# Queries of five of eight batches in three 16-bit terms, their normalised rows turned by transposing DMAs, in a fused attention and expert kernel

## The reference

```python
xn = layernorm(x)                               # (8, 256, 256), no gain
q1, q2 = xn @ q1_w.T, xn @ q2_w.T               # the queries of the change
k1, v  = ctx @ kv1_w.T;  k2 = first half of ctx @ kv2_w.T
a = softmax(q1 k1' / 4) - lam * softmax(q2 k2' / 4)
x = x + (rmsnorm(a v) * norm_w) @ proj_w.T + proj_b
x = x + experts(layernorm(x))
```

## Time and profile before

| | |
|---|---|
| median of three runs | 545.44 us (543.28 to 546.12) |
| the profiled execution | 542.85 us, of which the span of the trace is 541.1 us |
| busy share of the span | PE 91%, DVE 71%, ACT 63%, POOL 53% |
| mean granted clock of PE | 0.952 of full |
| data moved | 79.89 MB, DMA queue of SP busy 42.2% of 16 engines |

### The profile page before, as it was taken

One profiled execution on the slowest core, in us unless ns is written; L12 is line 12 of the kernel. 1 busy time (PEld: TensorE's weight loads), 2 busy tenths in 40 slices (PEclk: granted clock), 3 DMA queues, 4 the chain that ended last, 5 costly groups with the idle time before them and its releaser, 6 DMA issues.

```text
span 541.1 us, 12094 instructions
## 1 busy us (share of the span) xinstructions
PE 490.0 (91%) x3720; PEld 364.2 (67%) x3735; DVE 384.6 (71%) x816; ACT 339.7 (63%) x643; POOL 286.0 (53%) x364
## 2 busy tenths in 40 slices
PE   4976989999998988797999999999999999999990
PEld 3845556766765655445778788888888888777650
DVE  5664368998978857794888888888766677666551
ACT  2333688988888886353776777776565556545530
POOL 7332646566546454244146576556656655554244
PEclk9978599999999999697999999999999999999997
DMA  8668676876776534434546877896665555643224
GB/s 258 179 180 257 192 199 184 263 198 191 255 194 190 182 113 147 146 108 132 163 106 137 181 178 153 184 167 165 100 92 95 90 82 94 99 79 61 30 30 50
DMA packets 87883, 79.89 MB, mean 148 GB/s; under 512 B 48456, under 2 KB 73832, under 8 KB 87688
## 3 DMA queue, kind: packets, MB, share of 16 engines
q1 hardware_dynamic: 75900, 62.93, 42.2%
q0 software_dynamic: 11856, 16.16, 18.6%
q10 hardware_dynamic: 68, 0.03, 0.0%
HBM read 49.08 MB, written 22.41 MB: 132 GB/s over the span
## 4 chain that ended last, share of the span: by engine, by line
PE 60%; DMA 11%; DVE 8%; issue 6%; ACT 6%; SPq 6%; POOL 3%; ACTq 0%; POOLq 0%; DVEq 0%
PE bank L1540 26%; PE bank L1559 13%; PE bank L1346 4%; PE bank L1332 3%; SPq L496 3%; PE bank L1297 2%; DMA q_parts<-WE 2%; PE bank L1571 2%; DMA FB<-w 2%; PE bank L1369 2%; PE bank L1355 2%; DMA FB<-x_parts,slot_tok 2%; PE bank L1313 2%; DVE FB L1224 2%; POOL out L749 1%
## 5 line engine op out<-in xcount | busy, mean ns | idle before, releaser
L1540 PE MATMUL bank<-FB,WE 128*128 128x0 bf16 x1440 | 190.2, 283 | 2.4 <-issue 1.6
L1540 PEld LDWEIGHTS bank<-FB,WE 128*128 x1440 | 138.7, 99 | 34.7 <-issue 4.1
L749 POOL DMA_INDIRECT out<-FB,slot_tok x60 | 100.2, 1669 | 87.5 <-DVE FB L1241 82.6
L943 ACT ACTIVATE FB<-FB 128x512 bf16<-128x512 f32 x120 | 75.6, 630 | 68.0 <-DVE FB L1220 64.6
L1224 DVE TENSOR_TENSOR FB<-FB 128x512 bf16<-128x512 f32 x120 | 83.3, 694 | 43.3 <-ACT FB L943 38.6
L1559 PE MATMUL bank<-FB,WE 128*128 128x0 bf16 x720 | 103.5, 280 | 2.9 <-DVE FB L1224 2.4
L1220 DVE TENSOR_TENSOR FB<-FB,bank 128x512 f32<-128x512 f32 x120 | 82.0, 683 | 26.7 <-ACT FB L937 21.5
L937 ACT ACTIVATE FB<-bank 128x512 f32<-128x512 f32 x120 | 70.7, 589 | 34.4 <-PE bank L1540 26.2
L740 POOL DMA_INDIRECT FB<-x_parts,slot_tok x60 | 63.7, 1062 | 52.5 <-DMA FB<-FB 31.6
L1559 PEld LDWEIGHTS bank<-FB,WE 128*128 x720 | 67.7, 98 | 21.8 <-issue 6.3
L656 POOL TENSOR_TENSOR WE<-FB,WE 128x256 bf16<-128x256 f32 x104 | 67.8, 678 | 21.1 <-ACT WE L780 21.1
(11 more groups left out here) (181 smaller groups left out, 612.1 us busy)
## 6 DMA issues: line engine op xcount, KB each, us to landing
FB<-w SPq DMA_DIRECT2D x26, 512.0 KB, 5.4
WE<-w SPq DMA_DIRECT2D x44, 256.0 KB
WE<-q_parts SPq DMA_DIRECT2D x32, 200.0 KB
WE<-x SPq DMA_DIRECT2D x16, 256.0 KB, 5.6
q_parts<-FB SPq DMA_DIRECT2D x32, 128.0 KB
x_parts<-WE SPq DMA_DIRECT2D x20, 128.0 KB, 3.9
out<-WE SPq DMA_DIRECT2D x20, 128.0 KB, 5.0
q_parts<-WE SPq DMA_DIRECT2D x16, 128.0 KB
```

The source lines that it names most:

```text
L749: pool.indirect_dma_start(out=out, out_offset=bass.IndirectOffsetOnAxis(ap=slot_tok[:, c:c + 1].bitcast(U32), axis=0), in_=result_tile(c), ...
L943: nc.scalar.activation(hT[k % 3][:, 0, :], hid[k % 2], ACT.Copy).then_inc(hi_ready, 1)
L1540: ins = nc.tensor.matmul(to, wf[:, bass.ds(at + o, P)], xgT[s % 2][:, 2 * part + kc, :].shape_from_register(long[s % 2]), start=(z == 0), ...
```

## The change

For batches 3 to 7 (made in rounds 0 to 4) the 32-bit path is replaced:

- XT and XC go. ACT's new **NH** rounds xn to 16 bits (both tiles, 128 x 512 in all), POOL's new **NL** subtracts to get the low part (two instructions of 128 x 256), and SP's new **NT** issues two transposing DMAs of 128 x 512 16-bit elements, one for each tile, which write both parts into the place of xnT.
- Q is made of three 16-bit products (high by high, high by low, low by high): twelve matmuls of 256 columns for each half in the place of eight 32-bit instructions.
- The query weights are split once in the preparation: one ACT instruction of 128 x 1024 and four on POOL of 128 x 256.
- The tables are changed: LN goes from the eighth place of DVE's round to the fourth, NH stands behind E 3, NL between L 6 and L 7, NT behind W 0 and ahead of the second half's QOH and QOL, Q 0 moves behind S 13, QL 0 behind the two XL, both RS (the variances of LN) stand together. MT of all batches but the first uses bank 5 in the place of 6.

```diff
+            def turned_norm(b):
+                for t in range(TPB):
+                    sp.wait_ge(xnl_ready, TPB * (b - 3) + t + 1)
+                    sp.wait_ge(q_mm, 2 * b)
+                    sp.dma_start(xnT_parts[:, :, t * P:(t + 1) * P], xns[:, t].rearrange("p s (k f) -> p (s k) f", k=KC), transpose=True).then_inc(xn_turned[t], 16)
...
+            for k in range(KC):
+                for c in range(2):
+                    pool.wait_ge(wqh_ready, 1)
+                    part = slice(c * D, (c + 1) * D)
+                    whole = slice((2 * k + c) * D, (2 * k + c + 1) * D)
+                    nc.gpsimd.tensor_tensor(wqs[:, 1, whole], wq_sb[:, k, part], wqs[:, 0, whole], ALU.subtract).then_inc(wql_ready, 1)
...
+                if kind == "NL":
+                    for t in range(TPB):
+                        pool.wait_ge(xnh_ready, b - 2)
+                        nc.gpsimd.tensor_tensor(xns[:, t, 1, :], xn[:, t, :], xns[:, t, 0, :], ALU.subtract).then_inc(xnl_ready, 1)
...
+            def xn_hi(b):
+                act.wait_ge(xn_ready, TPB * (b + 1))
+                if b > 3:
+                    for t in range(TPB):
+                        act.wait_ge(xn_turned[t], 16 * (b - 3))
+                nc.scalar.activation(xns[:, :, 0, :], xn, ACT.Copy).then_inc(xnh_ready, 1)
...
+                terms = [(k, wpart, part) for k in range(KC) for wpart, part in ((0, 0), (0, 1), (1, 0))]
                 for half in range(2):
                     m = 2 * a + half
+                    if b >= 3:
+                        for z, (k, wpart, part) in enumerate(terms):
+                            ins = nc.tensor.matmul(A[:, half * S:(half + 1) * S], wqs[:, wpart, (4 * k + m) * P:(4 * k + m + 1) * P],
+                                                   xnT_parts[:, KC * part + k, :], start=(z == 0), stop=(z == len(terms) - 1))
+                        continue
...
-            ("QI", 1, 1), ("OX", 0, -3), ("OX", 1, -3), ("W", 2, 0), ("QOH", 0, 2), ("OO", 0, -2), ("XD", 0, -1), ("QOL", 0, 2), ("W", 0, 1),
+            ("QI", 1, 1), ("OX", 0, -3), ("OX", 1, -3), ("W", 2, 0), ("QOH", 0, 2), ("OO", 0, -2), ("XD", 0, -1), ("QOL", 0, 2), ("W", 0, 1), ("NT", 0, 3),
```

More of the change, by code:

```diff
@@ L129, in moe_attention_kernel @@
         lams = big(3 * H).rearrange("p (a h) -> p a h", a=3)
+        wqs = big(2 * KC * 2 * D, BF16).rearrange("p (s n) -> p s n", s=2)
         normw = big(KC)
@@ L133, in moe_attention_kernel @@
         xnT = att(KC * S).rearrange("p (k n) -> p k n", k=KC)
+        xnT_parts = xnT.rearrange("p k n -> p (k n)").bitcast(BF16).rearrange("p (c n) -> p c n", c=2 * KC)
         qh = att(4 * S, BF16).rearrange("p (m n) -> p m n", m=4)
@@ L202, in moe_attention_kernel @@
         pr = [tail[:, 2 * W1N + 1024 * n:2 * W1N + 1024 * (n + 1)].bitcast(F32) for n in range(4)] + [spare(512) for _ in range(4)]
+        xns = spare(TPB * 2 * D, BF16).rearrange("p (t s n) -> p t s n", t=TPB, s=2)
         late_stage = [tail[:, 2 * W1N + CH * n:2 * W1N + CH * (n + 1)].bitcast(F32) for n in range(LSTG)]
@@ L257, in moe_attention_kernel @@
         xn_ready = sem("xn_ready")
+        xnh_ready = sem("xnh_ready")
+        xnl_ready = sem("xnl_ready")
+        xn_turned = [sem(f"xn_turned{t}") for t in range(TPB)]
+        wqh_ready = sem("wqh_ready")
+        wql_ready = sem("wql_ready")
         xt_mm = sem("xt_mm")
@@ L364, in moe_attention_kernel @@
             ("L", 9, -1), ("L", 10, -1), ("L", 11, -1), ("L", 0, 0), ("RM", 1, -2), ("L", 1, 0), ("L", 2, 0), ("R2", 0, -2), ("R2", 1, -2),
-            ("L", 3, 0), ("RS", 0, 3), ("L", 4, 0), ("L", 5, 0), ("L", 6, 0), ("L", 7, 0), ("RS", 1, 3), ("RM", 0, -1), ("L", 8, 0))
+            ("L", 3, 0), ("RS", 0, 3), ("RS", 1, 3), ("L", 4, 0), ("L", 5, 0), ("L", 6, 0), ("NL", 0, 3), ("L", 7, 0), ("RM", 0, -1), ("L", 8, 0))
         SP_PLAN = (
-            ("QI", 1, 1), ("OX", 0, -3), ("OX", 1, -3), ("W", 2, 0), ("QOH", 0, 2), ("OO", 0, -2), ("XD", 0, -1), ("QOL", 0, 2), ("W", 0, 1),
+            ("QI", 1, 1), ("OX", 0, -3), ("OX", 1, -3), ("W", 2, 0), ("QOH", 0, 2), ("OO", 0, -2), ("XD", 0, -1), ("QOL", 0, 2), ("W", 0, 1), ("NT", 0, 3),
             ("OO", 1, -2), ("QOH", 1, 2), ("QOL", 1, 2), ("XA", 0, 4), ("W", 1, 1), ("QI", 0, 2), ("SH", 0, 1))
-        FIRST = {"XT": 3, "XC": 3, "Q": 3, "QH": 3, "QL": 2, "QOH": 2, "QOL": 2, "QI": 2, "LS": 4, "RS": 4, "LN": 4, "XA": 4, "SC": 1,
+        FIRST = {"NH": 3, "NL": 3, "NT": 3, "Q": 3, "QH": 3, "QL": 2, "QOH": 2, "QOL": 2, "QI": 2, "LS": 4, "RS": 4, "LN": 4, "XA": 4, "SC": 1,
                  "MX": 1, "W": 0}
@@ L589, in _ @@
                     queries_lo_out(b, i)
+                if kind == "NT":
+                    turned_norm(b)
                 if kind == "XA":
@@ L797, in mt_copy @@
                     act.wait_ge(m_in, 32 * b)
-                nc.scalar.activation(mT[0:64, :], A6[0:64, 0:S // 2].bitcast(BF16), ACT.Copy).then_inc(mT_ready, 1)
+                nc.scalar.activation(mT[0:64, :], (A6 if b == 0 else A5)[0:64, 0:S // 2].bitcast(BF16), ACT.Copy).then_inc(mT_ready, 1)
             def exp(b, h):
@@ L863, in _ @@
             values(3)
+            act.wait_ge(wq_in, 16 * KC)
+            nc.scalar.activation(wqs[:, 0, :], wq_sb.rearrange("p k n -> p (k n)"), ACT.Copy).then_inc(wqh_ready, 1)
             hi_part(0)
@@ L894, in _ @@
                     ots_copy(b, i)
-                if kind == "XC":
-                    xnT_copy(b)
+                if kind == "NH":
+                    xn_hi(b)
                 if kind == "QH":
@@ L988, in ln1_norm @@
                     dve.wait_ge(ln1_rstd, TPB * b + t + 1)
-                    if b > 0:
+                    if b > 3:
+                        dve.wait_ge(xnl_ready, TPB * (b - 3))
+                    elif b > 0:
                         dve.wait_ge(xt_mm, b)
@@ L1290, in queries @@
             def queries(b, a):
-                pe.wait_ge(wq_in, 16 * KC)
-                pe.wait_ge(xnT_ready, b + 1)
+                if b < 3:
+                    pe.wait_ge(wq_in, 16 * KC)
+                    pe.wait_ge(xnT_ready, b + 1)
+                else:
+                    pe.wait_ge(wql_ready, 4)
+                    for t in range(TPB):
+                        pe.wait_ge(xn_turned[t], 16 * (b - 2))
                 A = bank_for(6 + a, ql_ready, 2 * b + a + 1)
+                terms = [(k, wpart, part) for k in range(KC) for wpart, part in ((0, 0), (0, 1), (1, 0))]
                 for half in range(2):
                     m = 2 * a + half
+                    if b >= 3:
[3 more added lines that the diff above has]
+                        continue
                     for k in range(KC):
@@ L1318, in transposed_max @@
                 pe.wait_ge(mneg_ready, b + 1)
-                A = bank_for(6, mT_ready, b + 1)
+                A = bank_for(6 if b == 0 else 5, mT_ready, b + 1)
                 for t in range(TPB):
@@ L1454, in _ @@
                     weighted_values(b, i)
-                if kind == "XT":
-                    transposed_x(b)
                 if kind == "Q":
```

## The result

| | |
|---|---|
| median of four runs | 555.94 us (548.95 to 557.43), before 545.28 us |
| ratio to the kernel before | 1.0173 (95%: 1.0116 to 1.023), some 9.4 us |
| the profiled execution | 557.43 us, of which the span is 555.6 us |
| busy share of the span | PE 88%, DVE 69%, ACT 62%, POOL 53% |
| data moved | 81.21 MB, DMA queue of SP busy 44.0% of 16 engines |

What follows compares the result with a forecast made beforehand. PE bounds the rounds, with the queries' store and reload path right behind. At 20.5 us a round, four rounds cost +1.5 and the first +1.9: +3.4 on 542.85 gives 546.3 profiled, 548.8 on the median; range 540 to 557.5.

Steps and rivals of the forecast that it cites:

- The sign: Whole kernel: slower by more than half a per cent, chance 0.51; 0.29 for within half a per cent, 0.20 for faster.
- The mechanism that was named: SP's queue: NT ahead of the stores, and W 0 behind the late L 7, delay the queries; 20.5 us a round.
- two rivals at 557.4 and 555.6: Rounds with NT: store path in full, 557.4, or PE's clock falling before SC 0, 555.6; together chance 0.18.
- five rounds 8.0 us, all of it where PE is full: PE, rounds with NT: transposes gone and cheaper query products shed 1.59 us a round, 8.0 in five.
- the floor of 18.54 a round: PE: the length to which a round would fall if nothing but PE's lighter work held it.
- SP's path, steps 1 to 5: From SC 0 at T through LN, NH, NL, L 7, W 0, NT and QOL 1 to the next SC 0, at most T + 22.15.
- upper end of 22.15: Next SC 0 at T + 22.15 if stores land 4.94 and queries 5.77 us later, as in the round without queries.
- the middle that I took: 20.5 us a round, between 18.91 and 22.15, since DMA showed both a full and a half-empty stretch.
- The landings: Behind QOL 1: stores land in 4.94 us, queries in 5.77; how much of that is backlog decides the round.
- The faster one: Rounds: PE was the bound and the path shrinks with it, 18.91 us a round, 541.0 in all; chance 0.25.
- The path in full, or the clock falls: Rounds of T + 22.15, 557.4, or PE at half clock after idling, 1.7 us more a round, 555.6; chance 0.18.
- Q waits for its rows: Q 0 on PE: late transposes make it wait 1.6 us, round 20.1, +1 with the first round, 546; chance 0.12.

Runs made afterwards that it cites:

- the terms alone: Kernel before, rows still turned on PE and Q 0 in its old place, with the products of batches 3 to 7 in three 16-bit terms: ratio 1.0037.
- early_q: Changed kernel without NT, Q reading weight parts instead of turned rows, with Q 0, QH 0 and QL 0 back at their old places: ratio 0.9977 to the kernel before.
- no turns: Changed kernel without NT; Q takes parts of the weights in place of the turned rows, Q 0 still late: ratio 1.0125 to the kernel before.
- the idle turns: Kernel before plus two transposing transfers a round, same size and place on SP as NT, whose result nothing reads: ratio 1.007.
- NT, NL or both later: Changed kernel with NT behind XA on SP (1.0165), NL behind L 7 on POOL (median 553.14 us beside 543.66), or both moves (1.016).
- unread: Changed kernel with NT kept, but Q takes parts of the weights, so nothing reads the turned rows: ratio 1.0158 to the kernel before.

## Why the prediction was right, and where its reasons were wrong

The sign was right (0.51 on slower), and the measured 555.94 us lies in the range; the forecast of 548.8 was 7.1 us too low. Its place was right as well, the five rounds with NT. The sum had +1.9 us for the first round and +1.5 for the four behind it; the profiled execution has 4.24 and 9.7. The mechanism that was named is a part of it only, and the larger part was not in the sum. That the range holds the result is partly luck: its upper end was drawn for two rivals at 557.4 and 555.6, and neither is the main cause.

**PE.** The work was sized well: counted as the prediction did, without overlaps, the queries of the round from 122.16 take 2.63 us where 2 x 1.32 was taken and 3.65 stood before, and with XT's 0.59 PE sheds the 1.6 us that were forecast. The sentence that failed is "five rounds 8.0 us, all of it where PE is full"; the floor of 18.54 a round rests on it, the sum does not. That PE is busy in 19.92 of 20 us does not say that less work there shortens the round: the terms alone shed 1.0 us a round and gave 1.0037, and early_q shed 1.6 and gave 0.9977. The trace of before had the answer. Its round without queries takes 14.17 us from SC 0 to S 13, only 1.0 less than the 15.16 with XT and Q 0. I read that round as a whole, 18.91 us, and put its end down to the query path.

**The place of Q 0.** Costed at nothing; it was mentioned only as the time at which Q is due. It is the largest term: 1.0125 against 0.9977, 5.6 us by the medians and 8 by the ratios. The question to ask was what the steps on both sides of the moved one wait for, in the place that it leaves and in the place that it takes.

**SP's path, steps 1 to 5.** The steps themselves held. In the round from 122.16, NH ended at T + 4.33 (predicted 3.9), the two NL at T + 5.9 (5.2), L 7 at T + 6.5 (5.85), W 0 at T + 6.9 (6.35), NT at T + 9.5 (9.0), QOL 1 at T + 12.1 (11.45); the landings took 2.99 and 6.64 us in the place of 4.94 and 5.77, and SC 0 came at T + 21.73, near the upper end of 22.15 and not at the middle that I took. So in the changed kernel the path is a limit, with 0.45 to 1.51 us of idle PE before three SC 0. It is not the main cause of the loss: with QOL 1 back at T + 8.6 the ratio was 1.016 in the place of 1.0173, well within the intervals.

**The landings.** The stores landed in 2.99 us when issued later, which fits that the longer landing before was in part a backlog; no run shows that apart. The Trainium skill's count of engines for such a store ("DMA: Bandwidth & Descriptors", the section on why a DMA increments its semaphore by 16) had given T + 22 in the prediction, with landings as long as before. The round did end there, but not by that: the stores landed 1.95 us sooner, and later issue and a longer landing of the queries made up for it.

**The transfers.** 1.5 us of transfers for two transposes, from the expert stage, was too little: among loaded queues two took 1.9 us of 16 engines by the changed kernel against no turns, and 3.2 by the idle turns against before (last section). Their cost alone is 1.007, and on top of the late Q 0 it is the step from 1.0125 to 1.0173, within the two intervals. The Trainium skill's rule ("VectorE: DVE Perf Modes", rules for kernel authors) to turn a 128 x 128 block on TensorE where PSUM will do agrees with the runs: the same products with the turns on PE gave 1.0037, though most of the difference from 1.0173 is the place of Q 0. The change moved it because the rows come later: NT's second transpose is issued at some T + 8.2 and lands 4.4 us after, and the old Q 0 began at T + 11.9.

**The rivals.** The faster one is refuted: leaving the turning out altogether gave 549.43, and with Q 0 early 544.63, and neither came to its 541.0. "The path in full, or the clock falls" named 557.4 and 555.6, near the result, but with the path shortened most of the loss stayed, so its number is near for another reason. Its clock was seen in the first round, and in the fourth at 158.5 to 163 (0.51, above): DMA moved 23 GB/s from 154.5 to 156, a piece of weights landed late, ACT's H and E waited for it, and PE for E. In ACT's and PE's order of time:

```profile
156.34 1.06 ACT L806 ACTIVATE WE<-FB 128x1024 bf16<-128x1024 f32 x1 [1.48 <-DMA FB<-w]
```

```profile
158.23 0.41 PE L1380 MATMUL bank<-WE 128*77 128x256 bf16 x2 [1.44 <-ACT WE L838]
...
161.12 2.77 PE L1341 MATMUL bank<-FB,WE 128*128 128x256 bf16 x12
```

"Q waits for its rows" is there where SP's order is undone, 0.61 us.

Not settled: how much of the fourth round's 25.29 us belongs to the turns. The same round took 21.0 to 21.7 us with NT, NL or both later; single rounds of 23.59 (idle turns) and 25.83 us (unread) were seen in two other kernels with turns, but one of 22.50 in a kernel without. Nor was the transposing NT run with Q 0 in its early place, where Q 0 would wait for its rows.

## What to carry to other kernels

A busy share of 99% on one engine does not make its work the bound. Cut the round at the steps that a change moves, and compare each piece with a round that lacks the work: the difference is all that can be won by taking the work out. A step on an engine that is always busy may be there to cover the others' waits; before it is moved, look at what the engine would wait for in the place it leaves, and who waits for it in the place it takes.

## What the runs showed of the hardware that was not expected

A transposing DMA of 128 x 512 16-bit elements took more of the engines among loaded queues than the 0.75 us of the expert stage: 1.6 us of all 16 by the idle turns (12.7 us for eight, above), and 0.95 by the changed kernel against no turns, with 9.4% of 81 us for eight. From issue to landing it took 4.4 us (median), as the DMA issues of the changed kernel in 76 to 157 us show, where in the expert stage the first tile was back 2.8 us after its issue. The changed kernel, then no turns:

```profile
q1 hardware_dynamic: 18831, 16.56, 80.7%
...
FB<-w SPq DMA_DIRECT2D x12, 512.0 KB, 5.8
...
FB<-FB SPq DMA_TRANSPOSE x8, 4.4
```

```profile
q1 hardware_dynamic: 15954, 16.91, 71.3%
```

A plain copy of the same bytes held SP for 0.7 us in the place of 1.25.
